# Differential attention and a routed feed-forward layer on one core: transposes one step later, a copy out of PSUM behind the exponentials

## The reference, cut to what matters

```python
q, k, v = heads(x @ Wq), heads(x @ Wk), heads(x @ Wv)      # 16 query heads, 4 kv heads, 2 x 32 each
q1, q2, k1, k2 = halves(q), halves(k), rotated by position
a1 = softmax(q1 @ k1.T * scale + causal_mask)
a2 = softmax(q2 @ k2.T * scale + causal_mask)
out = (a1 - lam * a2) @ v                                   # lam: one number
out = (out - mean) * rsqrt(var + 1e-5) * gn_w + gn_b        # mean, var over all tokens of a batch and a head
x = layernorm(x + (out * 0.8) @ Wo)
x = layernorm(x + top2_of_8_experts(x))                     # routed feed-forward, width 352
```

## Time and profile before

| | us |
|---|---|
| three runs | 2258.5, 2269.7, 2272.9 |
| their median | 2269.7 |
| profiled execution | 2265.9 |
| its span, first to last instruction | 2264.1 |

### The profile page before, as it was taken

How to read it: one execution, slowest core, us unless ns; L and a number is a source line. 1 busy time by engine, 2 the same in 40 slices (tenths; PEclk the granted TensorE clock), 3 DMA queues, 4 the chain that set the end, 5 groups by cost and what they waited for, 6 DMA issues and landing times. The chain is left out here.

```text
span 2264.1 us, 37174 instructions
## 1 busy us (share of the span) xinstructions
PE 1808.6 (80%) x9826; PEld 1336.3 (59%) x9827; DVE 1458.3 (64%) x3278; ACT 1129.6 (50%) x3263; POOL 614.6 (27%) x504
## 2 busy tenths in 40 slices
PE   3678898898889879879888888967099999999700
PEld 3455555656655755655655564544099999999600
DVE  2588867878788788787787878751333333333366
ACT  1466756667566575676667766661122222222133
POOL 2222312412231242241232223110542222200165
PEclk7788898899889889799989989988599999999855
DMA  7855534545454463453545455320543333223288
GB/s 262 282 139 152 145 99 140 178 112 149 134 166 120 126 200 114 124 174 103 159 151 147 129 152 168 75 75 19 181 146 112 112 114 120 74 83 98 73 269 269
DMA packets 142837, 319.51 MB, mean 141 GB/s; under 512 B 16704, under 2 KB 19264, under 8 KB 140512
## 3 DMA queue, kind: packets, MB, share of 16 engines
q1 hardware_dynamic: 113280, 241.84, 37.8%
q0 software_dynamic: 14432, 48.64, 6.4%
q10 hardware_dynamic: 14976, 27.27, 3.2%
HBM read 215.97 MB, written 109.05 MB: 144 GB/s over the span
## 5 line engine op out<-in xcount | busy, mean ns | idle before, releaser
L735 ACT ACTIVATE expd<-S,neg_max 128x128 f32<-128x128 f32 (+3 forms) x1024 | 530.7, 534 | 158.7 <-DVE neg_max L878 156.2
L878 DVE TENSOR_REDUCE neg_max<-S 128x2 f32<-128x768 f32 (+3 forms) x384 | 399.7, 1041 | 278.9 <-PE S L598 277.5
L909 DVE SCALAR_TENSOR_TENSOR mixed<-expd,rho 128x384 f32<-128x384 f32 (+3 forms) x512 | 337.2, 678 | 0.3 <-issue 0.3
L747 ACT ACTIVATE probsT<-PTp 128x512 f32<-128x512 f32 (+2 forms) x384 | 203.7, 531 | 254.0 <-PE PTp L609 251.3
L490 POOL TENSOR_TENSOR swapped<-swapped,rope_t 128x512 f32<-128x512 f32 x80 | 103.3, 1291 | 767.2 <-DVE swapped L864 767.2
L594 PE MATMUL S<-kT,qT 128*128 128x256 f32 (+2 forms) x1024 | 285.8, 382 | 27.4 <-DMA qT<-parts_rows 13.4
L609 PE MATMUL PTp<-ident,mixed 128*128 128x128 f32 x1280 | 221.3, 290 | 102.3 <-DVE mixed L909 99.7
L644 PE MATMUL tail<-wo,ctxT 128*128 128x512 f32 x512 | 252.9, 622 | 24.9 <-ACT ctxT L779 22.2
L594 PEld LDWEIGHTS S<-kT,qT 128*128 128x128 f32 x1024 | 165.7, 199 | 127.5 <-issue 82.4
L1311 ACT ACTIVATE xT_hi<-xTp 128x512 fp32r<-128x512 f32 x72 | 43.1, 599 | 359.2 <-DVE yo L1487 348.9
L609 PEld LDWEIGHTS PTp<-ident,mixed 128*128 128x128 f32 x1280 | 145.3, 148 | 126.6 <-DVE mixed L909 123.5
(11 more groups left out here) (206 smaller groups left out, 3631.1 us busy)
## 6 DMA issues: line engine op xcount, KB each, us to landing
qT<-parts_rows SPq DMA_DIRECT2D x256, 256.0 KB, 4.6
parts_rows<-parts SPq DMA_DIRECT2D x160, 256.0 KB, 2.0
wqk<-wqk_split SPq DMA_DIRECT2D x75, 512.0 KB, 5.2
xin<-expert_in_rows SPq DMA_DIRECT2D x72, 256.0 KB, 2.9
expert_out_rows<-yo ACTq DMA_DIRECT2D x72, 256.0 KB, 3.2
kT<-parts_rows SPq DMA_DIRECT2D x64, 256.0 KB, 4.3
x<-in_x SPq DMA_DIRECT2D x8, 1024.0 KB, 7.8
x_rows<-x SPq DMA_DIRECT2D x8, 1024.0 KB, 7.0
```

Of the source, the lines that this page charges most:

```text
L735: ex = nc.scalar.activation(expd[s % 3][:, k * slot:k * slot + w], S[s % 2][:, k * slot:k * slot + w], ACT.Exp, bias=neg_max[s % 3][:, k:k ...
L747: nc.scalar.activation(probsT[i % 2][:, 0:i + 1, half:half + n, pair, :].rearrange("p j a q -> p a j q"), PTp[:, 0:w].rearrange("p (a j q) ...
L878: nc.vector.tensor_reduce(neg_max[s % 3][:, 0:k], v, AX, ALU.max, negate=True).then_inc(max_ready, 1)
L909: ins = nc.vector.scalar_tensor_tensor(out=mixed[sl % 3][:, a * 256:a * 256 + w], in0=e2, scalar=rr[:, i, h:h + 1], in1=e1, op0=ALU.mult, ...
```

## The change

Transposes, and with them `take_probsT`, `values`, `take_scale`, `scaled_out`, `chunk_stats` and GpSimd's `take_vals` of the last kv group, move one step later, for all of them are placed by the two lags. Their order within a step stays, but for ScalarE: `take_scale` comes behind `take_probsT` and `exps`. The diff is whole:

```diff
-LAG_T, LAG_V = 3, 4
+LAG_T, LAG_V = 4, 5
...
             def body(b, par, first, last):
                 for s, kv, u in steps(b, first, last):
-                    if (s - LAG_V - 1) % NU in LAST_OF and lagged(b, s, LAG_V + 1, first):
-                        take_scale(tile_no(b, s, LAG_V + 1))
                     if lagged(b, s, LAG_T, first):
                         take_probsT(*lagged(b, s, LAG_T, first), tile_no(b, s, LAG_T))
                     exps(s, u)
+                    if (s - LAG_V - 1) % NU in LAST_OF and lagged(b, s, LAG_V + 1, first):
+                        take_scale(tile_no(b, s, LAG_V + 1))
                     if (s - 2) % NU in LAST_OF and lagged(b, s, 2, first):
                         widen(*lagged(b, s, 2, first), tile_no(b, s, 2))
```

## The result

The changed kernel takes 2343.5 us in the median of four runs (2342.4 to 2344.6), the kernel before 2270.9 beside it: a ratio of 1.033 (1.031 to 1.035). I had said 2289 and at most 2318. It is slower, where I had given most to "within 1%" and 0.37 to slower.

A forecast was written before the change was run, and what follows sets the result against it. No engine was full overall (TensorE 80% busy); stretches of full TensorE alternate with stretches of full VectorE or ScalarE. Seven batches at +3.3 (+23) and batch 0 at -3 give +20 on 2265.9: 2286, plus 3.8, predicted 2289; range 2230 to 2318.

The forecast's parts named there:

- (3): ScalarE's copy out of O moved behind the exponentials: given nothing; without cover at most 14 us a batch.
- (b): Step 10: the multiply now stands before VectorE's maxima, which start 1.1 us late; 1.2 us carried.
- (e): Steps 21 to 40: TensorE, then VectorE, is full and neither gives anything back; 5.3 us carried.
- (1): Transposes one step later find their mix done: TensorE's 99.7 us of waits on mixed probabilities go.
- (a): Steps 7 and 8: the multiply stands behind the statistics, TensorE waits for it; step 9 is 0.6 us late.
- (c): Steps 15 to 17: last tile's values come behind the output projection, no longer beside the norm wait; 3.5 us late.
- (d): Steps 19 to 21: statistics in VectorE's step 19 delay the multiply, TensorE waits 1.9 us; step 21 5.4 us late.
- (f): Steps 41 to 47: the 2.74 us wait on routing work goes; part is lost again in step 46; 2.0 us gained.
- B: Rival, clearly slower: same places, but the clock falls at both long waits; +6.9 us a batch, 2315 us; chance 0.22.
- A: Rival, faster: TensorE keeps its lead, only the norm's 1.2 us lost, tail at full clock; 2233 us; chance 0.20.
- C: Rival, no change: VectorE's order decides everywhere, what (c) and (d) lose comes back in (f); 2270 us; chance 0.14.
- D: Rival: TensorE's gaps are the path itself, 99.7 us go and nothing comes back; 2170 us; chance 0.04.

The follow-up runs named there:

- `lags_only`: Changed kernel with ScalarE's copy out of O back at the head of its step, new distances 4 and 5 kept: 2298.6 us, ratio 1.014.
- `cov3`: Changed kernel with the values of each group's last tile (tile 3) alone ahead of the tail task in TensorE's step: 2323.9 us, ratio 1.024.
- `stats_early`: Changed kernel with the statistics of a kv group one step earlier, back in steps 6, 18, 30 and 42: 2338.1 us, ratio 1.031.
- `cov2`: Changed kernel with the values of each group's third tile (tile 2) alone ahead of the tail task in TensorE's step: 2318.5 us, ratio 1.022.
- `head1`: Changed kernel with the copy of tile 1 alone at the head of ScalarE's step, the others behind the exponentials: 2307.1 us, ratio 1.019.
- `lags_cover`: Changed kernel with all copies at the head of ScalarE's step and values of tiles 2 and 3 ahead of the tail task: 2260.2 us, ratio 0.997.
- `two_repairs`: Changed kernel with tile 1's copy at the head and values of tiles 2 and 3 ahead of the tail task: 2275.2 us, ratio 1.002.
- `before_cover`: Kernel before, distances 3 and 4, with the values of tiles 2 and 3 ahead of the tail task: 2244.5 us, ratio 0.989.
- `transposes_only`: Kernel before with only the transposes one step later (distances 4 and 4), copy at the head of its step: 2289.4 us, ratio 1.006.

## Why the prediction was wrong

The sum had + 3.3 us a batch, and + 12.1 were measured. The step that failed most is (3): the copy behind the exponentials was put at nothing and costs 45 us at the new distances. Without it (`lags_only`) the kernel is 30 us over before, where the other terms of the sum gave 20. In the walk through the batch, (b) and (e) failed next: 1.2 us carried to step 13 where the trace shows 5.1, and nothing from step 21 to 41 where it shows 3.0.

**What bounds the kernel.** Right in kind: a wait that goes pays only where it does not come back on the same slow engine. It came back on ScalarE, which I had at 50% busy and did not walk through.

**(1)** The wait on the mixed values went to nothing, and "the step's own scores, which need the exponentials of two steps before, or the values product" are what is late next: both, 69.3 and 46.6 us (8.9 and 35.4 before).

**(a)** The wait at step 8 is there (3.02 us for 2.7), and up to step 9 the batch is late by 0.9 (15.3 + 14.9 against 18.1 + 14.8, less 1.8) for a forecast 0.6. But 1.0 stood in steps 0 to 5 already, so the size is luck.

**(b)** I carried 1.2 us to step 13; it is 5.1 (0.9 + 4.2). This is the first step that failed. The stretch at half clock by the wait for the scaled output (809.6 to 816.4 before, 843.9 to 850.8 after) now reaches over step 9, which takes TensorE 4.3 us (846.98 to 851.27) instead of 2.4 (817.25 to 819.69). So the maxima of step 10 start at 852.89, by the batch's own time 2.9 us late (the 1.8 moved taken off) where I had 1.1, and TensorE waits for the exponentials behind them (2.01 us). Then come the wait behind ScalarE's table load (1.11) and a second stretch at half; before, 2.2 us of waits on the mixed values stood here. I had walked VectorE through these steps and neither ScalarE nor the clock.

**(c)** Right in place, and near in size: +2.3 forecast from step 13 to 17 (1.2 to 3.5), +1.6 measured, with a wait for the norm of 2.85 us where I had said 4 to 5, since TensorE was late as well. `cov3` shows the price of the place, 20 us over all places of tile 3's values.

**(d)** Right in size: +1.9 forecast from step 17 to 21, +2.3 measured. The wait has another name, L644 on L966 and not L622 on L917. That the statistics cause it is not a loss by itself: in `stats_early` that wait falls from 1.8 to 0.7 us in batch 4, and the whole is 5 us less, within what the two intervals leave open.

**(e)** I let 5.3 be carried through steps 21 to 40 with nothing lost. It was 9.0 at step 21 and 12.0 at 41. TensorE was full to step 31, but in step 32 stands a wait of 2.06 us for the scaled output, and in steps 33 to 37 come those behind the copy and for the transposed rows.

**(f)** The gain is there and larger: the wait at 948.59 is gone, and steps 41 to 43 take 6.8 us less, where I had 3.2 (2.7 and 0.5). The missing 3.6 are the clock: 10.7 us at 1.2 GHz before, none after, and TensorE's busy time in these steps goes from 9.4 to 5.3 us. My "if the missing wait leaves it at 2.4 GHz, 5.6 us a batch come back" stood among the bounds and was not in the sum. Then 2.8 + 1.8 go again by the batch's end, with a wait of 2.75 us for a copy of ScalarE's (vnext) and one of 3.75 for the exponentials in front of the next batch's first scores (2.44 us of idle stood there before); I had charged 1.2. Net 2.2 for my 2.0, so the size of the net is luck: both of its parts are far larger.

**(3)** "I give it nothing" is the term that cost most. I looked at the length of the copy (0.4 us) and its idle time before. What moved is its end: from early in ScalarE's step to behind two exponentials and, in step 33, a table load, with the multiply and the maxima of VectorE behind. I bounded it by 0.9 us, 16 times a batch, 14 us; the price, 45 us or 6.4 a batch, lies within that bound, but for tile 1, 36 us of it, the traces put it at one delay of 1.05 us in step 33 and the clock behind it, not at four of 0.9. The clock is no fixed part of that price: `cov2` wins back the same stretch with the copy left where it is.

**Batch 0**: - 3 forecast, - 4.8 measured. **The sum**: + 3.3 a batch forecast, + 9.9 in batch 4 and + 12.1 in the mean of batches 1 to 7. (2286 + 3.8 is 2290, not 2289.)

**Rivals.** B (2315, the clock falls at the long waits) named a mechanism that took part, but it is small in the net: with 40 us more at 1.2 GHz in the stage, TensorE's busy time grew by only 3.9 us (1808.6 to 1812.5): much of the added time lies on waits, and the clock gives back in steps 41 to 43 (4.1 us of busy time in batch 4) what it takes in steps 9 to 13 (3.2); the rest is waiting. B was still too small, for its base lacked (3), and it looked for the clock at steps 16 and 20: by the table it fell for longer at 9 to 13 and at 13 to 17 (7.2 and 3.4 us more), and not at 20. A and C fell with the first row. D, the gaps as the path itself, is answered by numbers: "Perfetto Trace Analysis", section Optimization Strategy, of the Trainium skill advises to find the gaps of the most-contended engine and make what ends them come sooner. Here 99.7 us of such gaps went and the kernel lost 73, and the fastest kernel of the study keeps them (98.8).

What stays open: why the copy costs 18 us at the old distances, where no run takes it apart by tile; why the last batch grew by 18.1 us, half as much again as the others; and through which steps the other three tiles' copies cost their 11. Open too is why the clock stays up at the batch's ends once both repairs are in. And no run changes the clock alone: that it makes up most of the price of the copy is read from TensorE's busy time and the granted clock, not from an experiment of its own.

## What to carry to other kernels

When a stage of work is moved one step on, walk the engines that look idle too, and for each moved instruction ask when it ends and who stands behind it, not how long it takes: a copy of 0.4 us, four times a batch, cost 36 us, most of it where it ended behind a table load: 1 us of delay, with half clock behind it. Independent work belongs ahead of a wait in the program order of the engine, where it fills it; behind it, it only adds, and the order of two blocks in TensorE's step was worth 25 us to the untouched kernel, with its largest wait still in place. Move it one tile at a time, since the same order for all tiles lost 24 us where it met a bank not yet free.

## What the runs showed of the hardware

The same wait can be followed by either clock. TensorE in step 4 to 5, first in the kernel after, then in `head1`:

```profile
826.22 0.62 PE L594 MATMUL S<-kT,qT 128*128 128x384 f32 x2 [2.40 <-ACT expd L735]
...
827.64 0.63 PE L577 MATMUL prep<-xl,wqk 128*128 128x512 f32 x1
```

```profile
807.49 0.62 PE L594 MATMUL S<-kT,qT 128*128 128x384 f32 x2 [2.40 <-ACT expd L735]
...
808.55 0.39 PE L577 MATMUL prep<-xl,wqk 128*128 128x512 f32 x1
```

The engine did the same work before it in this batch (8.1 us for steps 0 to 3 in both) and waited the same 2.40 us; the clock fell behind it in the one (0.63 us a matmul) and not in the other (0.39). That alone makes 1.6 us in this batch (steps 3 to 5: 10.0 against 8.4). Within `head1` it differs by batch too: it does not fall there in batches 2 and 4 and falls in 3 and 5. So these rows don't let the price of the clock be read off the wait in front of it, and a sum over seven batches should carry it as a range. Over the kernels of the study the time at half clock in the stage follows the kernel's time only roughly: 247 us in `lags_cover` (2260), 258 in `two_repairs` (2275), 281 in `before_cover` (2245), 350 in `transposes_only` (2289) and in the changed kernel (2343).
